# Four load buffers for the weight statistics, an earlier residual load and normalisation, and a reordered attention loop in a transformer layer on eight cores

## The reference

```
q, k, v = x @ Wq.T, x @ Wk.T, x @ Wv.T
s = 30 * tanh((q . k / 8) / 30), masked to j <= i and j > i - 1024
x = layernorm(x + softmax(s) @ v @ Wo.T)
quantize(W) = clip(round(W / (mean(|W|) + 1e-5)), -1, 1)
h = relu(x @ quantize(W1).T + b1);  out = h @ quantize(W2).T + b2
x = layernorm(x + out)
```

## Time and profile before

| | us |
|---|---|
| median of 3 runs (lowest, highest) | 1924.34 (1921.14, 1925.15) |
| the profiled execution, its own time | 1924.06 |
| span of its slowest core, core 1 | 1922.5 |
| spans of the other cores | 1885.3 to 1917.3 |
| busy in the span: TensorE, ScalarE, VectorE, GpSimd | 1273.5, 743.8, 581.1, 217.6 |
| mean DMA rate of core 1 | 97 GB/s |

### The profile page before, as it was taken

The page is one execution under the profiler, slowest core; times in us unless marked ns, Lnnn a source line. Parts: engine busy times, 40 slices in busy tenths (PEclk is TensorE's granted clock), DMA queues, the critical chain, the costliest instruction groups (busy, mean ns, idle before and its releaser), DMA issues. The chain is left out here.

```text
span 1922.5 us, 24006 instructions; the slowest of 8 cores (1885.3 to 1922.5 us)
## 1 busy us (share of the span) xinstructions
PE 1273.5 (66%) x8196; PEld 707.1 (37%) x8196; DVE 581.1 (30%) x751; ACT 743.8 (39%) x667; POOL 217.6 (11%) x261
## 2 busy tenths in 40 slices
PE   4693067787767776767776108961777799567771
PEld 2352045555545454545544003420232244222230
DVE  0234433445444444454445360021101100020211
ACT  1231068887767676767760003320101033101110
POOL 1000000000000000000001110026000000440404
PEclk9797567778767777777778558985777799877896
DMA  9776632232323233232323452240212122332311
GB/s 146 167 199 181 193 80 68 81 94 83 89 80 94 81 88 94 77 92 80 88 77 112 126 160 78 75 135 0 88 66 88 39 61 77 110 134 85 111 64 44
DMA packets 128597, 186.68 MB, mean 97 GB/s; under 512 B 11104, under 2 KB 95072, under 8 KB 124384
## 3 DMA queue, kind: packets, MB, share of 16 engines
q1 hardware_dynamic: 105936, 133.24, 23.1%
q0 software_dynamic: 22544, 51.91, 10.4%
HBM read 161.53 MB, written 35.65 MB: 103 GB/s over the span
## 5 line engine op out<-in xcount | busy, mean ns | idle before, releaser
L532 PE MATMUL spsP<-QT,KTd 64*128 64x128 bf16 x2304 | 181.9, 233 | 226.1 <-ACT Tst L549 154.6
L549 ACT ACTIVATE Tst<-spsP 128x1024 f32<-128x1024 f32 x256 | 262.2, 1024 | 178.6 <-PE spsP L540 149.5
L1066 PE MATMUL f2ps<-hT,w2b 128*128 128x512 bf16 x1024 | 288.3, 451 | 5.7 <-DMA w2b<-w2q_t 4.7
L1020 PE MATMUL f1ps<-x2bf,w1b 128*128 128x512 bf16 x1024 | 226.5, 385 | 93.6 <-DVE x2bf L977 93.6
L568 ACT ACTIVATE Pst<-Tst,cm 128x4608 bf16<-128x4608 f32 x64 | 264.7, 4136 | 13.5 <-ACT Tst L555 13.3
L624 DVE RECIPROCAL den_sb<-pvd 128x256 f32<-128x256 f32 x64 | 112.5, 1757 | 358.9 <-PE pvd L608 354.1
L532 PEld LDWEIGHTS spsP<-QT,KTd 64*128 64x128 bf16 x2304 | 98.8, 98 | 299.9 <-issue 283.3
L592 PE MATMUL pvd<-Pst,Vv 128*64 128x256 bf16 x1152 | 196.1, 409 | 1.9 <-DVE OTn L632 1.9
L1066 PEld LDWEIGHTS f2ps<-hT,w2b 128*128 128x128 bf16 x1024 | 116.6, 114 | 181.0 <-issue 103.0
L1020 PEld LDWEIGHTS f1ps<-x2bf,w1b 128*128 128x128 bf16 x1024 | 101.4, 99 | 218.7 <-issue 101.3
L1093 ACT CAST t_bf<-x 128x512 bf16<-128x512 f32 x32 | 19.8, 618 | 409.1 <-DVE x L1086 409.1
(11 more groups left out here) (77 smaller groups left out, 967.3 us busy)
## 6 DMA issues: line engine op xcount, KB each, us to landing
qin<-w1T SPq DMA_DIRECT2D x64, 512.0 KB, 4.8
qin<-w2T SPq DMA_DIRECT2D x64, 512.0 KB, 4.6
w2b<-w2q_t SPq DMA_DIRECT2D x32, 1024.0 KB, 5.1
w1b<-w1q_t SPq DMA_DIRECT2D x64, 256.0 KB, 2.6
w1q_t<-qout POOLq DMA_DIRECT2D x32, 256.0 KB, 4.2
r1d<-r1f POOLq DMA_DIRECT2D x64, 128.0 KB, 4.9
w2q_t<-qout POOLq DMA_DIRECT2D x32, 256.0 KB, 4.3
outT<-x POOLq DMA_DIRECT2D x4, 2048.0 KB, 8.0
```

Source lines behind the costliest of these rows:

```text
L532: sp=last_in_bank: e.matmul(ps[:, col:col + 128], lhsT, rhs, start=st, stop=sp),
L549: lambda e, ps=ps, kbp=kbp: e.activation(Tst[:, kbp * 1024:(kbp + 1) * 1024], ps[:, 0:1024], AF.Tanh, scale=1.0 / 240.0),
L1020: lambda e, dc=dc, nt=nt, wslot=wslot, pslot=pslot: e.matmul(f1ps[pslot][:, :], w1b[wslot][:, dc * 128:(dc + 1) * 128], x2bf[:, dc * 1024 ...
L1066: lambda e, fc=fc, nt=nt, wslot=wslot, pslot=pslot: e.matmul(f2ps[pslot][:, :], w2b[wslot][:, fc * 128:(fc + 1) * 128], hT[:, fc * 1024 + ...
```

## The change

- `qin` has four buffers in place of two. The load of index i waits for index i-4, and four loads are issued ahead of phase 1's first reduction.
- The two stores of stage D go over the gpsimd queue and a semaphore of their own, MRS. On the gpsimd queue they stand ahead of the `r1d` store of the same pump.
- In each round of phase 2 `quant_pump(g)` and `wo_pump(g)` are emitted ahead of `emit_scores_acts(g)`.
- The loads of `mean4`, `rstd4` and `x2`, and `emit_norm_cast(0, 0)`, stand ahead of the barrier of phase 2, behind the last quantisation step. The buffers they write lie where phase 2's K, V, Q, validity table and load buffers were, so the loads wait for the last round's matmuls (pvT), and the VectorE part waits for the last quantisation. The barrier does not wait for the landing of `x2`, but each engine has to reach it.

```diff
@@ -33,9 +33,9 @@
 class Sched:
 
     SEM_NAMES = ("T", "V", "A", "G", "BAR", "LDS", "GW", "XB0", "XB1",
-                 "QI0", "QI1", "QO0", "QO1", "W10", "W11", "W12",
+                 "QI0", "QI1", "QI2", "QI3", "QO0", "QO1", "W10", "W11", "W12",
                  "W20", "W21", "W22", "OST", "XR0", "XR1", "XR2", "XR3", "R1S0", "R1S1",
-                 "RL", "RLG", "MRL")
+                 "RL", "RLG", "MRL", "MRS")
 
     def __init__(self, nc, es):
         self.nc = nc
@@ -172,7 +172,7 @@
             Vv = sb12("Vv", [128, CTXCH * 256], BF16)
             QT = sb12("QT", [128, DCH * QTOK], BF16)
             vrep_sb = sb12("vrep_sb", [128, CTXCH * 128], BF16)
-            qin = [sb12(f"qin{i}", [128, 1024], F32) for i in range(2)]
+            qin = [sb12(f"qin{i}", [128, 1024], F32) for i in range(4)]
             qx = sb12("qx", [128, 1024], BF16)
             qout = [sb12(f"qout{i}", [128, 1024], BF16) for i in range(2)]
             mean_all = sb12("mean_all", [128, QTOK], F32)
@@ -230,16 +230,16 @@
                     i = st1["issued"]
                     if i >= NQ1:
                         return
-                    if i >= 2:
-                        assert q1_red_done[i - 2] > 0
-                        waits = (("V", q1_red_done[i - 2]),)
+                    if i >= 4:
+                        assert q1_red_done[i - 4] > 0
+                        waits = (("V", q1_red_done[i - 4]),)
                     else:
                         waits = ()
                     src, nsub = p1_steps[i]
-                    dst = qin[i % 2][:, :]
+                    dst = qin[i % 4][:, :]
                     if nsub > 1:
                         dst = dst.rearrange("p (a d) -> p a d", a=nsub)
-                    q1_dma_done[i] = S.dma("sync", dst, src, f"QI{i % 2}", waits=waits)
+                    q1_dma_done[i] = S.dma("sync", dst, src, f"QI{i % 4}", waits=waits)
                     st1["issued"] += 1
 
                 def q1_reduce():
@@ -249,14 +249,14 @@
                     S.do("vector",
                          lambda e, i=i: e.tensor_reduce(
                              qred[:, i * 8:(i + 1) * 8],
-                             qin[i % 2][:].rearrange("p (a x) -> p a x", a=8),
+                             qin[i % 4][:].rearrange("p (a x) -> p a x", a=8),
                              AX.X, ALU.add, apply_absolute_value=True),
-                         waits=((f"QI{i % 2}", q1_dma_done[i]),), incs=(("V", 1),))
+                         waits=((f"QI{i % 4}", q1_dma_done[i]),), incs=(("V", 1),))
                     q1_red_done[i] = S.c["V"]
                     st1["reduced"] += 1
 
-                q1_issue()
-                q1_issue()
+                for _ in range(4):
+                    q1_issue()
 
                 xb_dma_done = [0] * 8
                 kps_evac = [0, 0]
@@ -376,18 +376,18 @@
                     kind, idx = q2[i]
                     if kind == "w1":
                         src = w1T_q[:, :, idx * 128:(idx + 1) * 128]
-                        dst = qin[i % 2][:].rearrange("p (a f) -> p a f", a=DCH)
+                        dst = qin[i % 4][:].rearrange("p (a f) -> p a f", a=DCH)
                     else:
                         fq, dc = idx // 8, idx % 8
                         src = w2T_q[:, fq, :, dc * 128:(dc + 1) * 128]
-                        dst = qin[i % 2][:].rearrange("p (a f) -> p a f", a=8)
-                    if i >= 2:
-                        assert q2_cmp_done[i - 2] > 0
-                        waits = (("V", q2_cmp_done[i - 2]),)
+                        dst = qin[i % 4][:].rearrange("p (a f) -> p a f", a=8)
+                    if i >= 4:
+                        assert q2_cmp_done[i - 4] > 0
+                        waits = (("V", q2_cmp_done[i - 4]),)
                     else:
                         assert v_th_box[0] > 0
                         waits = (("V", v_th_box[0]),)
-                    q2_dma_done[i] = S.dma("sync", dst, src, f"QI{i % 2}", waits=waits)
+                    q2_dma_done[i] = S.dma("sync", dst, src, f"QI{i % 4}", waits=waits)
                     st2["issued"] += 1
 
                 def q2_step():
@@ -397,16 +397,16 @@
                     kind, idx = q2[i]
                     neg = nth1 if kind == "w1" else nth2
                     pos = th1 if kind == "w1" else th2
-                    waits = [(f"QI{i % 2}", q2_dma_done[i])]
+                    waits = [(f"QI{i % 4}", q2_dma_done[i])]
                     if i >= 2:
                         waits.append((f"QO{i % 2}", q2_out_done[i - 2]))
                     S.do("vector",
                          lambda e, i=i, neg=neg: e.tensor_single_scalar(
-                             qx[:, :], qin[i % 2][:, :], neg[:, :], ALU.is_lt),
+                             qx[:, :], qin[i % 4][:, :], neg[:, :], ALU.is_lt),
                          waits=tuple(waits), incs=(("V", 1),))
                     S.do("vector",
                          lambda e, i=i, pos=pos: e.scalar_tensor_tensor(
-                             qout[i % 2][:, :], qin[i % 2][:, :], pos[:, :],
+                             qout[i % 2][:, :], qin[i % 4][:, :], pos[:, :],
                              qx[:, :], ALU.is_gt, ALU.subtract),
                          incs=(("V", 1),))
                     q2_cmp_done[i] = S.c["V"]
@@ -759,12 +760,13 @@
                         den_sb[:, 256:512], ALU.mult, ALU.subtract),
                         incs=(("V", 1),))
                     last_extr_V[0] = S.c["V"]
-                    S.dma("sync", meand[:, c0:c0 + 256],
-                          mean_all[:, c0:c0 + 256], "MRL",
+                    S.dma("gpsimd", meand[:, c0:c0 + 256],
+                          mean_all[:, c0:c0 + 256], "MRS",
                           waits=(("V", last_extr_V[0]),))
-                    S.dma("sync", rstdd[:, c0:c0 + 256],
-                          rstd_all[:, c0:c0 + 256], "MRL",
+                    S.dma("gpsimd", rstdd[:, c0:c0 + 256],
+                          rstd_all[:, c0:c0 + 256], "MRS",
                           waits=(("V", last_extr_V[0]),))
+                    mrs_after[(k, half)] = S.c["MRS"]
 
                 def wo_pump(i):
                     uA = i - 17
@@ -786,13 +788,13 @@
                     if fold_on and g < DCH:
                         wo_gd[0] = S.dma("gpsimd", wo_bf_r[:, g, :],
                                          woT_r[:, g, :], "GW")
+                    quant_pump(g)
+                    if fold_on:
+                        wo_pump(g)
                     emit_scores_acts(g)
                     if g >= 1:
                         emit_pv(g - 1)
                         emit_norm(g - 1)
-                    quant_pump(g)
-                    if fold_on:
-                        wo_pump(g)
                 _ng = NG if p2_ng is None else p2_ng
                 emit_pv(_ng - 1)
                 emit_norm(_ng - 1)
@@ -809,40 +811,117 @@
                     q2_issue()
                 qo_final = (S.c["QO0"], S.c["QO1"])
 
-                if fold_on:
-                    for fc in range(2):
-                        w1_pre[fc] = S.dma(
-                            "sync", w1b[fc][:, :], w1q_t[fc], f"W1{fc}",
-                            waits=(("QO0", qo_final[0]), ("QO1", qo_final[1])))
-
-                S.barrier(drain=("QI0", "QI1", "QO0", "QO1", "LDS", "GW",
-                                 "XR0", "XR1", "XR2", "XR3", "MRL",
-                                 "R1S0", "R1S1"))
...
         otn_ctx.close()
         x2 = sb("x2", [128, DCH * QTOK], F32)
+        mean4 = sb("mean4", [128, 1024], F32)
+        rstd4 = sb("rstd4", [128, 1024], F32)
+        f_tmp = sb("f_tmp", [128, 512], F32)
+        sig_sb = sb("sig_sb4", [128, 512], F32)
+        x2bf = sb("x2bf", [128, DCH * 1024], BF16)
+        x2_r = x2[:].rearrange("p (dc c) -> p dc c", dc=DCH)
+        BDRAIN = ("QI0", "QI1", "QI2", "QI3", "QO0", "QO1", "LDS", "GW",
+                  "XR0", "XR1", "XR2", "XR3", "MRS", "R1S0", "R1S1")
+
...
+        pvT = pv_done[_ng - 1]
+        S.dma("sync", mean4[:, :], meand[:, 0:1024], "MRL",
+              waits=(("T", pvT), ("MRS", mrs_after[(1, 1)])))
+        mrl_cnt = [0, 0]
+        mrl_cnt[0] = S.dma("sync", rstd4[:, :], rstdd[:, 0:1024], "MRL")
+        rl_tot = {}
+        for t in (0, 1):
+            for dc in range(DCH):
+                eng, q = (("sync", "RL") if (t == 0 and dc % 2 == 0)
+                          else ("gpsimd", "RLG"))
+                w = ()
+                if dc == 0 or (t == 0 and dc == 1):
+                    w = (("T", pvT),
+                         ("R1S0", r1s_cnt[30 if t == 0 else 62]),
+                         ("R1S1", r1s_cnt[31 if t == 0 else 63]))
+                S.dma(eng, x2_r[:, dc, t * 1024:(t + 1) * 1024],
+                      r1d_r[:, dc, t * 1024:(t + 1) * 1024], q, waits=w)
+            rl_tot[t] = (S.c["RL"], S.c["RLG"])
+
+        g_norm = [0, 0]
+
```

(37 more changed lines are left out.)

104 lines of the change are left out of this document (49 added, 55 removed).

## The result

The changed kernel takes 1881.64 us (median of nine runs, 1872.85 to 1947.19); the kernel before, run beside it, 1924.02 us (ten runs). The ratio is 0.9775 with a 95% interval of 0.9752 to 0.9798: 2.25% faster. The three longest executions (1911.84 to 1947.19) fell in a slower state, in which the cores of one die or of both have a lower granted clock; every ratio here leaves such executions out. The profiled execution took 1882.74 us.

What follows compares the result with a forecast made beforehand. The prediction took load latency in phase 1, TensorE's round in the loop and the stretch from stage D to f1ps as bounds: 1922.5 - 50 + 9 - 12 = 1869.5, with 1.6 us around it 1871 us, range 1845 to 1897.

Steps and rivals of the forecast that it cites:

- What bounds phase 1: Phase 1: a chain of load latencies, not full DMA engines; four buffers end it at 182 us, gaining 50 us.
- the 64 us that it would have made: Phase 1: estimated gain in place of 50 us if a core's loads ran at the skill page's 358 GB/s.
- loads outrun TensorE: Phase 1 rival, 22%: at 1.4 us a load the projections end the phase; gain 68 us, time 1853.
- half full: Phase 1 rival, 13%: a load costs 2.1 us of DMA time with four in flight; gain 27 us, time 1894.
- The reordered round: Phase 2 loop: stage A waits 3.0 us for the norm at rounds 17, 33 and 49; 9 us lost.
- the bound that the prediction had at 14: Phase 2 loop: upper loss if TensorE's clock stays at 1.2 GHz for a round after each window-start wait.
- The stores of stage D on gpsimd: Calls after the loop: chained stores hold up r1d stores, 2.7 us at each of two stage Ds; 5.4 us lost.
- The early residual: Last stage D to f1ps: earlier loads and normalisation; 80.1 us, Td's delay included, against 92.0; 12 us gained.
- Td: The end of the last stage D, from which later marks are counted; predicted 5.4 us later than before.
- Passing the barrier takes 2.0 us: Barrier between phase 2 and the feed-forward: priced at 2.0 us from phase 1's end, putting f1ps at Td + 74.7.
- The warning on VectorE and GpSimd: Behind stage D: VectorE's fast copies may delay GpSimd's descriptor writing; four delays of 2.5 us would take 10 of 12 us.
- From there to the end the program is unchanged, and I count it as unchanged: From f1ps to the end of the kernel: 763.6 us, counted as 0 change.

Runs made afterwards that it cites:

- experiments 6, 7 and 12: 6: changed kernel, second-half x2 loads behind the barrier, 1883.15 us; 7: changed kernel without the block end before the feed-forward, 1890.66 us; 12: early_with_block_end, 1888.86 us.
- combined: Changed kernel with projection behind the norm, late stage D stores and first-half x2 loads (after unit 55's stage D) on ScalarE's queue, no block end: 1869.99 us.
- after: The changed kernel itself, with the whole change, against the kernel before: 1881.64 us, ratio 0.9775.
- only_wo_moved_back: Changed kernel with only the output projection's calls (wo_pump) back behind the norm, quantising still ahead of the scores: 1853.94 us, ratio 0.9619.
- early_with_block_end: Changed kernel with projection behind the norm, late stores and early first-half x2 loads on ScalarE's queue, block end behind the second-half load issues: 1888.86 us.

## Why the prediction held, and where its steps failed

**What bounds phase 1: right.** Last reduction predicted near 182 us, measured 182.3; share above 0.9, measured 0.94 to 0.96 until the projections end and 0.89 behind, just under it; gain predicted 50 us, measured 52.0 in the median of the cores and 54.6 with the buffers alone. The starting point was 7 us off (first reduction at 68.5, not 61.5, as four loads share the engines), and the load's price was off the other way: between 160 and 181 us 6.14 MB, 11.7 loads, took 87.6% of 21 us, 1.57 us a load and not 1.72. The two errors nearly cancel (56 loads at 0.15 us less are 8.4 us), which is luck. By the Trainium skill, "DMA: Bandwidth & Descriptors", section Specifications, a core can have about 358 GB/s; the windows of 15 to 25 us here reach 303 GB/s at most and stay under the page's figure, and the 64 us that it would have made did not come. The rivals "loads outrun TensorE" and "half full" both fell.

**The reordered round: right in mechanism, the term of 9 us measured 13.1.** Three waits for `OTn` of 9.9 us in all, at rounds 17, 33 and 49 only. The rest is the bound that the prediction had at 14: behind each wait the granted clock is lower, 0.61, 0.61 and 0.71 over 16 us. The statement that the cycle is otherwise the same is right for the pair of calls, but it closed my eyes to the fact that the two calls alone are worth different things: the quantising ahead gains 12 us, the projection ahead then loses 25.

**The stores of stage D on gpsimd: right in mechanism, 5.4 us predicted for the tail, 9.3 measured.** The chain itself cost 3.9; the prediction had no term for the rest, of which the `qin` loads in the tail may be a part (not shown). Prediction and measurement agree that it is lost time.

**The early residual: the step that failed.** From stage D to f1ps 74.7 us were predicted, 84.3 came on core 0. By the prediction's own marks (Td is 1038.77): last quantising step ends at Td + 20.8 (19.7 said); first `x2` load Td + 22.1 (20.7); normalisation begins Td + 45.4 (40.7), because the four loads took 23.3 us, the first two 7.9 and 7.0 us beside SyncE's own loads, where 5.0 was taken; last cast ends Td + 77.4 (72.5); f1ps Td + 84.3 (74.7). So the sum slipped by 4.9 us up to the cast, and by another 4.7 at **"Passing the barrier takes 2.0 us"**. That sentence took the price from the end of phase 1, which is the same kind of boundary (a barrier with an `S.flush` behind it), as if every such boundary cost the same. Part of the price is GpSimd's DRAIN, and that took 0.81 us there, where GpSimd had issued 9 transfers, and 4.8 us here, behind 164 (experiments 6, 7 and 12). The change itself made it longer: its `x2` loads and stage D stores were put on GpSimd's queue ahead of the boundary, and the DRAIN there had been 2.17 us before. The same boundary had been there before, between the last quantising store (1092.93) and the first `x2` load (1099.81) in the earlier trace rows: 6.9 us, 2.1 of them the landing of that store, that the prediction read as part of the old path and then did not carry to the new one. The change moved the boundary, it did not take it away. The third part is the base: the 92.0 us of the page were core 1's, the longest of the eight; their median was 86.9. Against that the change gained 1.6 us, where the prediction had 17.3 (and 5.4 to pay).

**The warning on VectorE and GpSimd.** With VectorE idle and another queue issuing, the loads of `x2` go no faster (4.8 us each in combined) than from GpSimd beside a busy VectorE (4.5 in after). The Trainium skill, "SBUF — State Buffer", section "SBUF: two separate sides", was read as 10 us of loss through VectorE holding up GpSimd's descriptor writing; the pace of these loads shows no sign of it. Whether a single store near stage D was held, no run tells.

**"From there to the end the program is unchanged, and I count it as unchanged": true of the program, not of its time.** It gave 3.5 us back in after, within what the cores differ by (744 to 764 us before), and took up to 16 us more than before in the experiments. About 1 us of what it gave back is the last DRAIN of GpSimd (0.37 us in place of 1.35), as the `x2` loads now stand in the block ahead.

**The sum.** On the slowest cores 1922.5 became 1881.1, 41.4 us less, against 53 predicted; in the median of the cores 37.1. By the medians of the stages the misses are 15.7 us at the early residual, 4.1 at the round and 3.9 in the tail, against 2.0 more from phase 1 and 3.5 from the last stage. That it shows as only 11 us in the time is luck: the core that was slowest before (763.6 us behind f1ps) is not the slowest after.

**The better version.** only_wo_moved_back, 1853.94 us and 3.8% faster than before, differs from the change in one moved call.

## What to carry to other kernels

A stage that leaves the DMA engines at a share of 0.6 with everyone waiting for one load at a time is bound by loads in flight: a third buffer brought its end forward by 36 us and a fourth by another 16. A boundary where all engines meet must be priced where it stands, with everything that the slowest queue still has to issue ahead of it and with the DRAIN that GpSimd runs for the transfers it has issued; a change that moves it has to carry its price along, and taking a block end out only moves that DRAIN to the next one. And two calls moved together are tried one by one: here one gained 12 us and the other lost 25.

## What the runs showed of the hardware that was not expected

- The end of a program block costs what GpSimd's DRAIN takes there, and that grows with the transfers that GpSimd has issued in the block: 0.37 us for 4, 1.35 for 16, 3.48 for 156, 4.5 to 4.8 for 164 with the last one not yet landed. With the block end left out, 4.46 us came at the end of the kernel. It also waits for queues whose work nobody needs: 40.5 us in early_with_block_end.
- A TensorE stall of 3.24 us in the loop cost 6.0 us, as the granted clock stood at 0.61 in the stretch that holds it and the instructions behind it ran at up to 1.8 times their length.
- The same pass of the feed-forward takes 214, 223, 224 or 233 us from kernel to kernel, in groups from 10.8 us (granted clock 1.00) to 13.6 us and more (0.75 to 0.79), with the same pattern in all cores of a kernel, whenever they reach it. A gain of 27 us ahead of it can shrink to nothing in the total, so an edit ahead of such a pass is judged by its stage and by the total, and the two can disagree.
